# Two transformer-like layers on one core: when the third group's keys are sent, who sums two of eight output pairs, half a gram product, and eight tail tiles ahead of the experts

## What is computed

```python
xn = layernorm(x)
x  = x + causal_attention_16_heads(xn, w_qkv, w_o) + moe_top2_of_16(xn, Wg, bias, W1, W2)
xn = layernorm(x)
# second layer: no softmax; q and k are divided by their norms over all tokens
q, k, v = split(xn @ W + b)
qn, kn  = q / norm(q, over tokens), k / norm(k, over tokens)
attn    = qn * sum(kn * v, over tokens)                  # one row of 256 for all tokens
moe     = sum over the 4 best of 16 experts: weight * (silu(xn @ we1) * (xn @ we3)) @ we2
shared  = (silu(xn @ ws1) * (xn @ ws3)) @ ws2
x  = x + attn + shared / 5 + moe * 4 / 5
```

## Time and profile before

| | us |
|---|---|
| median of 3 runs | 906.23 (905.91 to 911.66) |
| the profiled execution | 906.89 |
| its span, first to last instruction | 905.2 |
| TensorE busy | 830.5 (92%) |
| VectorE busy | 645.3 (71%) |
| ScalarE busy | 468.8 (52%) |
| GpSimd busy | 437.1 (48%) |

### The profile page before, as it was taken

One profiled execution on the slowest core, in us unless ns is written; L12 is line 12 of the kernel. 1 busy time (PEld: TensorE's weight loads), 2 busy tenths in 40 slices (PEclk: granted clock), 3 DMA queues, 4 the chain that ended last, 5 costly groups with the idle time before them and its releaser, 6 DMA issues. The chain is left out here.

```text
span 905.2 us, 16683 instructions
## 1 busy us (share of the span) xinstructions
PE 830.5 (92%) x4934; PEld 449.4 (50%) x4935; DVE 645.3 (71%) x1472; ACT 468.8 (52%) x883; POOL 437.1 (48%) x720
## 2 busy tenths in 40 slices
PE   5978699999988999999999998989999989999993
PEld 3533133334533444444444432138644769888982
DVE  5587988898867888888788888437547336555648
ACT  2643154556654666666565666754313046555547
POOL 3422045603652433653435446531578848878820
PEclk9997698999998999999999999989999989999997
DMA  9654772210272121272211222325852235555566
GB/s 328 212 129 137 207 142 89 89 46 25 81 128 71 49 61 56 80 127 71 70 38 38 55 60 76 93 65 188 302 166 88 88 117 164 157 154 159 158 255 246
DMA packets 70182, 110.05 MB, mean 122 GB/s; under 512 B 16662, under 2 KB 49942, under 8 KB 69590
## 3 DMA queue, kind: packets, MB, share of 16 engines
q1 hardware_dynamic: 49430, 54.04, 22.9%
q0 software_dynamic: 16000, 45.70, 14.7%
q10 hardware_dynamic: 4672, 9.34, 3.4%
HBM read 62.53 MB, written 46.22 MB: 120 GB/s over the span
## 5 line engine op out<-in xcount | busy, mean ns | idle before, releaser
L1275 DVE TENSOR_REDUCE part_max<-ps_row 128x1 f32<-128x512 f32 (+3 forms) x560 | 353.6, 670 | 71.1 <-PE ps_row L1429 38.7
L1139 ACT ACTIVATE probs<-ps_st 128x1024 f32<-128x1024 f32 (+3 forms) x320 | 278.2, 896 | 204.6 <-PE ps_st L1408 188.2
L1333 PE MATMUL ps_o<-probs,v_all 128*17 128x512 f32 (+3 forms) x1280 | 150.4, 542 | 6.9 <-POOL probs L1009 5.6
L1429 PE MATMUL ps_row<-ks,qs 96*128 96x512 bf16 (+3 forms) x320 | 110.2, 379 | 13.7 <-DVE part_max L1275 9.3
L1429 PE MATMUL ps_row<-xt_ks,qs 96*128 96x512 bf16 (+3 forms) x320 | 104.5, 354 | 6.9 <-DVE part_max L1275 6.5
L1682 POOL DMA_INDIRECT yd<-moe_ys,moe_home x79 | 82.6, 1046 | 25.5 <-POOL moe_home L1676 13.4
L1408 PE MATMUL ps_st<-qs,ks 99*128 99x512 bf16 (+3 forms) x320 | 88.7, 360 | 2.9 <-DMA qs<-max_parts 2.7
L1408 PE MATMUL ps_st<-qs,xt_ks 99*128 99x512 bf16 (+3 forms) x320 | 85.7, 356 | 3.9 <-ACT probs L1139 2.8
L1702 PE MATMUL moe_ps_h<-moe_xs_t,moe_w_now 128*128 128x128 f32 x632 | 86.0, 280 | 1.3 <-ACT moe_xs_t L1607 0.8
L1702 PEld LDWEIGHTS moe_ps_h<-moe_xs_t,moe_w_now 128*128 128x128 f32 x632 | 78.4, 195 | 3.2 <-DVE moe_w_now L1569 2.0
L1429 PEld LDWEIGHTS ps_row<-ks,qs 96*128 96x128 bf16 x320 | 31.9, 100 | 95.6 <-DVE part_max L1275 52.8
(11 more groups left out here) (288 smaller groups left out, 1307.3 us busy)
## 6 DMA issues: line engine op xcount, KB each, us to landing
moe_xs<-xd SPq DMA_DIRECT2D x79, 129.0 KB
qk_parts<-probs SPq DMA_DIRECT2D x16, 384.0 KB, 4.2
qs<-qk_parts SPq DMA_DIRECT2D x96, 64.0 KB, 2.5
moe_xs<-xd POOLq DMA_DIRECT2D x47, 128.0 KB, 2.4
yd<-moe_ys POOLq DMA_DIRECT2D x47, 128.0 KB, 2.1
xd<-zeros POOLq DMA_DIRECT2D x2, 2048.0 KB, 15.5
moe_w<-in_w ACTq DMA_DIRECT2D x2, 2048.0 KB
w<-in_we SPq DMA_DIRECT2D x8, 512.0 KB
```

Source lines behind the costliest of these rows:

```text
L1139: act.activation(probs[:, at % NPB, :, off:CH], ps_st[at % 2][:, :, off:CH], ACT.Exp, scale=HD ** -0.5).then_inc(exp_done, 1)
L1275: dve.tensor_reduce(part_max[reduced % 2][:, h:h + k, i, j:j + 1], bank[:, 0:k * w].rearrange("p (h w) -> p h w", h=k), AX_X, ALU.max).the ...
L1333: mm = pe.matmul(ps_o[32 * q:32 * q + HD + 1, off:CH], m.v_all[:, k, g * HG + q, :], probs[:, (at + q // 2) % NPB, q % 2, off:CH], start=F ...
L1429: mm = pe.matmul(cols, qs[c][0:KROWS, h, i * P:(i + 1) * P], ks[g % 2][0:KROWS, h, j * CH:j * CH + w], start=True, stop=(j < c))
```

## The change

- SP sends the third group's keys (g = 2, buffer `ks`) right behind the unit `spread` of share 1, in place of `turn` (1, 2). Groups 1 and 3 are sent where they were.
- At the end, for the pairs 2 and 3 (`SUMMED`) ScalarE scales all four sets of blocks as before, but TensorE sums them: four products with a matrix that holds 5 on its diagonal (`five`), made by GpSimd at the start of the block, since the closing addition divides by 5. For the six other pairs ScalarE scales three sets and VectorE multiplies and adds the fourth itself (two instructions of 128 x 256). Loads and scalings go in the order of `LAST_LOADS`, additions and stores in that of `LAST_ADDS`, TensorE's work in that of `LAST_TAILS`.
- The gram product of the second half k = 1 leaves out its left 128 columns; they are the transpose of a part of the first half, which TensorE transposes and ScalarE copies after the gram. The product of the gram with the weights is done for k = 1 first, then for k = 0.
- `TAIL_FIRST` is 8: the tail of tiles 6 and 7 is computed in the second block too, in the bank `ps_o`. In the third block three pairs have a tail.

The diff, cut to its core:

```diff
@@ -882,6 +882,12 @@

+            def keys_of(g):
+                if g >= 2:
+                    sp.wait_ge(pv_done, last_pv(g - 2, C - 1))
+                load_keys(sp, m, g, slice(0, S), k_in[g % 2])
             load_first_group(sp, m, C - 1)
@@ -907,16 +913,16 @@
                     spread_divisors(sp, m, u[1])
+                    if SHARES[u[1]] == (0, 1):
+                        keys_of(2)
                 elif u[0] == "turn":
                     g, c = u[1:3]
                     if n:
                         rows_out(sp, n, c)
                     n += 1
-                    if g + 1 < NG and c == (1 if g == 0 else 2):
-                        if g >= 1:
-                            sp.wait_ge(pv_done, last_pv(g - 1, C - 1))
-                        load_keys(sp, m, g + 1, slice(0, S), k_in[(g + 1) % 2])
+                    if (g, c) in ((0, 1), (2, 2)):
+                        keys_of(g + 1)
                     if (g, c) == (1, 0):
@@ -1539,10 +1545,12 @@
         tail_done, finished = l.sem("moe1_tail_done"), l.sem("moe1_finished")
-        scaled = l.sem("moe1_scaled")
+        scaled, five_ready = l.sem("moe1_scaled"), l.sem("moe1_five_ready")
+        five = l.sb("moe1_five", [P, P])
         yg_pair = [yg8[:, 2 * n:2 * n + 2, :, :] for n in range(T // 4)] + [
             spare4[:, 2 * n:2 * n + 2, :, :] for n in range(T // 8)] + [last4[:, 2 * n:2 * n + 2, :, :] for n in range(T // 8)]
         step_sem = l.sem("moe1_dve")
+        by_act = [(n, k) for n in LAST_LOADS for k in range(top if n in SUMMED else top - 1)]
         block = ctx.enter_context(nc.Block())
@@ -1587,10 +1595,10 @@
                 sp.wait_ge(y_out[b], 16 * len(range(b, tiles, U)))
-            for n in range(T // 2):
+            for n in LAST_LOADS:
                 sp.dma_start(yg[2 * n], rows_of(2 * n)).then_inc(fetched[n], 16)
-            for n in range(T // 2):
-                sp.wait_ge(finished, n + 1)
+            for at, n in enumerate(LAST_ADDS):
+                sp.wait_ge(finished, at + 1)
                 sp.dma_start(out[0, 2 * n * P:2 * (n + 1) * P, :].rearrange("(i p) d -> p i d", p=P),
@@ -1617,11 +1625,11 @@
                 act.wait_ge(y_out[b], 16 * len(range(b, tiles, U)))
-            for n in range(T // 2):
+            for n in LAST_LOADS:
                 act.dma_start(yg[2 * n + 1], rows_of(2 * n + 1)).then_inc(fetched[n], 16)
-            for n in range(T // 2):
+            for n in LAST_LOADS:
                 act.wait_ge(fetched[n], 32)
-                for k in range(top):
+                for k in (k for pair, k in by_act if pair == n):
                     for i in (2 * n, 2 * n + 1):
@@ -1653,20 +1661,27 @@
             step = Steps(dve, step_sem)
-            for n in range(T // 2):
+            for n in LAST_ADDS:
                 both = m.x[:, 2 * n:2 * n + 2, :]
-                for k in range(top):
-                    dve.wait_ge(scaled, n * top + k + 1)
-                    step.then(dve.tensor_tensor(both, yg_pair[n][:, :, k, :], both, ALU.add))
-                if 2 * n < TAIL_FIRST:
-                    dve.sem_inc(finished, 1)
-                else:
-                    dve.wait_ge(tail_done, n + 1 - TAIL_FIRST // 2)
+                if n not in SUMMED:
+                    for k in range(top - 1):
+                        dve.wait_ge(scaled, by_act.index((n, k)) + 1)
+                        step.then(dve.tensor_tensor(both, yg_pair[n][:, :, k, :], both, ALU.add))
+                    dve.wait_ge(fetched[n], 32)
+                    for i in (2 * n, 2 * n + 1):
+                        step(dve.scalar_tensor_tensor(m.x[:, i, :], yg[i][:, top - 1, :], m.r["weight"][:, i, top - 1:top],
+                                                      m.x[:, i, :], ALU.mult, ALU.add))
+                    step.sync()
+                if n in LAST_TAILS:
+                    dve.wait_ge(tail_done, LAST_TAILS.index(n) + 1)
                     dve.scalar_tensor_tensor(both, ps_tail[n].rearrange("p (i d) -> p i d", d=D), 1.0 / (TOP1 + 1), both,
                                              ALU.mult, ALU.add).then_inc(finished, 1)
+                else:
+                    dve.sem_inc(finished, 1)

         @block.gpsimd
         def _(pool):
+            pool.tensor_scalar(five[:, :], m.ident[:, :], float(TOP1 + 1), None, ALU.mult).then_inc(five_ready, 1)
             step = Steps(pool, pool_sem)
@@ -1715,15 +1730,27 @@
             pe.wait_ge(hid_ready, tiles)
-            for n in range(TAIL_FIRST // 2, T // 2):
+            pe.wait_ge(five_ready, 1)
+            for n in LAST_TAILS:
+                bank = ps_tail[n]
                 if n == T // 2 - 2:
                     pe.wait_ge(y_copied, tiles)
                 for i in (2 * n, 2 * n + 1):
-                    mm = shared_tail(pe, m, ps_tail[n], i)
+                    if n not in SUMMED:
+                        mm = shared_tail(pe, m, bank, i)
+                        continue
+                    for k in range(top):
+                        pe.wait_ge(scaled, by_act.index((n, k)) + 1)
+                        mm = pe.matmul(bank[:, i % 2 * D:(i % 2 + 1) * D], five[:, :], yg[i][:, k, :],
+                                       start=(k == 0), stop=(k == top - 1))
                 mm.then_inc(tail_done, 1)


-TAIL_FIRST, TAIL_BEFORE = 6, 14
+TAIL_FIRST, TAIL_BEFORE = 8, 14
+SUMMED = (2, 3)
+LAST_LOADS = (0, 1, 2, 4, 5, 3, 6, 7)
+LAST_ADDS = (0, 1, 4, 2, 5, 6, 3, 7)
+LAST_TAILS = (4, 5, 6, 2, 7, 3)
 ROOT_BEFORE = 7
@@ -1756,11 +1783,11 @@
         banks_g = [l.ps(f"ps_gram{b}", [P, CH]) for b in range(KH)]
-        ps_g = [b[:, 0:DP] for b in banks_g]
+        ps_g = [b[:, k * P:DP] for k, b in enumerate(banks_g)]
         bank_l = l.ps("ps_l2", [P, CH])
         ps_ab = [l.ps(f"ps_ab{b}", [P, CH]) for b in range(2)]
         ps_o = l.ps("ps_o2", [P, 2, D])
-        ps_tail = [banks_g[1], banks_g[0], bank_l]
+        ps_tail = [banks_g[1][:, :], banks_g[0][:, :], bank_l[:, :], ps_o[:, :, :].rearrange("p i d -> p (i d)")]
         ps_gw, ps_sums, ps_ones = banks_g, bank_l, banks_g[0]
@@ -1881,7 +1908,9 @@
             for k in range(KH):
-                act.copy(gram[:, k, :], ps_g[k]).then_inc(gram_copied, 1)
+                act.copy(gram[:, k, k * P:DP], ps_g[k]).then_inc(gram_copied, 1)
+            act.wait_ge(gram_done, 2)
+            act.copy(gram[:, 1, 0:P], banks_g[0][:, 0:P]).then_inc(xt_ready, 1)
             act.wait_ge(logit_ready, 1)
@@ -1999,8 +2028,8 @@
                 dve.wait_ge(b_in, 16)
-                for k in range(KH):
-                    dve.wait_ge(gw_done, k + 1)
+                for k in (1, 0):
+                    dve.wait_ge(gw_done, KH - k)
                     step(dve.tensor_tensor(prod[:, k, 0:2 * D], ps_gw[k][:, :], w[:, k, 0:2 * D], ALU.mult))
@@ -2080,7 +2109,7 @@
                 pair = m.x[:, 2 * b:2 * b + 2, :]
-                step(dve.scalar_tensor_tensor(pair, bank[:, :].rearrange("p (i d) -> p i d", d=D), 1.0 / (TOP1 + 1), pair,
+                step(dve.scalar_tensor_tensor(pair, bank.rearrange("p (i d) -> p i d", d=D), 1.0 / (TOP1 + 1), pair,
                                               ALU.mult, ALU.add))
@@ -2115,7 +2144,7 @@
                     for k in range(KH):
-                        mm = pe.matmul(ps_g[k], xn[:, i, k * P:(k + 1) * P], xn[:, i, 0:DP],
+                        mm = pe.matmul(ps_g[k], xn[:, i, k * P:(k + 1) * P], xn[:, i, k * P:DP],
                                        start=(i == 0), stop=(i == T - 1))
@@ -2186,7 +2215,10 @@
             pe.wait_ge(gram_copied, KH)
-            for k in range(KH):
+            pe.transpose(banks_g[0][:, 0:P], gram[:, 0, P:2 * P], m.ident[:, :]).then_inc(gram_done, 1)
+            for k in (1, 0):
+                if k == 0:
+                    pe.wait_ge(xt_ready, T + 1)
                 for j in range(KH):
                     mm = pe.matmul(ps_gw[k][:, :], gram[:, j, k * P:(k + 1) * P], w[:, j, 0:2 * D],
                                    start=(j == 0), stop=(j == KH - 1))

```

## The result

The changed kernel is slower by 0.6%: over 15 runs of each, interleaved on one chip, the ratio of its time to that of the kernel before is 1.0059, 95% interval 1.0035 to 1.0084 (medians 915.62 and 907.40 us; executions in a disturbed state of the chip are in the medians and left out of the ratio). That is +3.2 to +7.6 us; forecast were +7.9, with "within 1%" as the likeliest class and 909.0 to 918.5 us as the range. On 906.23 us the ratio gives 911.6 us: class and range hold, and the point lies 2.5 us too high. The profiled execution after took 910.74 us, span 909.0, against 906.89 and 905.2.

The account below looks back on a forecast made before the run. TensorE was taken to bound attention, and the chain load, scale, add, store the end. Keys +9.9, boundary +0.4 and end -2.4 made +7.9 on 906.2: 914.1 us, range 909.0 to 918.5 us.

Parts of the forecast that it names:

- Part 1, the keys: Attention: later third-group keys remove TensorE's 6.0 us stop but add one of 15.9 us, net +9.9 us (+1.3 to +11.3).
- The rival of the fast keys: Attention: with TensorE stopped, keys land 5.7 us after first issue, new stop 7.3 us, total 905.5 us; chance 0.09.
- the 5.6 us: Attention: time for the six key loads by the skill's rule, 2.0 us plus bytes at 436 GB/s, making the edit nearly free.
- The old stop: Attention, kernel before: TensorE stands 6.00 us until 274.19 because the first divisors' gather queues behind six key loads; expected to go.
- the slow stretches behind the two stops cancel: Attention: TensorE's half-clock time after the new stop taken as long as after the old, worth 2.6 us, so no net term.
- Part 2, the half gram: Second block: shorter gram passes save 3.5 us of TensorE, of which -2.1 us net is kept (0 to -3.3).
- Part 3, the tail tiles: End of second block: two more tiles add 5.2 us of TensorE, using up VectorE's cover before SP's last load; +0.4 us (0 to +2.8).
- the cover of 2.6 us is used up, +0.4 us: Second block's end: VectorE's last product moves from 727.98 to 731.1 against SP's last load at 730.61, costing +0.4 us.
- Part 4, the end: Last stretch: less scaling and adding, ScalarE fed by the loads, VectorE ends at 900.1 instead of 902.59; -2.4 us.
- The rival of full length: Keys take their 15.7 us (+11.3), boundary +1.5, end gives 2.0: +10.8, total 917.0 us; chance 0.17.
- that of no gain at the end: Last stretch: pairs 2 and 3 wait on ScalarE and TensorE, VectorE idles what it saves; total 916.5 us; chance 0.10.
- that of no stop: Attention: SP reaches the spread earlier, so the new TensorE stop does not happen; total 895.6 us; chance 0.04.

Follow-up runs that it names:

- the first three groups: Three of four follow-up sets of kernels, each measured together with the kernel before, which took 907 to 918 us in the first and 896 to 897 in the others.
- the pair of the third group: The kernel before and the changed kernel, both measured again together: ratios 0.9997 and 1.0078, medians 896.72 and 904.95 us.
- the first group: Changed kernel with third group's keys at the old place, 0.999; kernel before with the keys' edit alone, 1.002; changed kernel with keys behind the first gather, 0.989.
- the second and third group: Sets with kernel before plus idle products (0.9993), eight tail tiles (1.0018) or half gram (0.9985), changed kernel unsummed (1.0110); then both kernels, each also with keys behind first gather (0.9858, 0.9866).
- the run without sums: Changed kernel with no pair summed by TensorE, pairs in the order 0 to 7: ratio to the kernel before 1.0110 [1.0085, 1.0135].
- The second measurement: The changed kernel unaltered, measured again against the kernel before: ratio 1.0078 [1.0052, 1.0104], median 904.95 us.

## Why the prediction was right, and where it was not

**Part 1, the keys: right.** The two terms are 16.11 and 6.00 us; I had 15.9 and 6.0. The landing took 14.4 us, and I had 14.3. That it came so close is partly luck: the two instances gave 15.7 and 15.5 us, and the 1.3 us that I took off for the experts' traffic came from no row. That these loads fill the DMA engines by themselves is shown by the rows with all compute engines stopped. The rival of the fast keys falls, and with it the 5.6 us. The Trainium skill (DMA: Bandwidth & Descriptors, Anatomy of one DMA) states the rule behind those 5.6 us for one DMA of GpSimd's path; these are six on SP's queue, and their 14.4 us don't agree with it. Three more profiles with this edit, one of each of the first three groups, have stops of 15.66, 16.30 and 17.01 us. The old stop is less steady, 4.45 to 7.36 us over the six profiles that have it. That the slow stretches behind the two stops cancel holds nearly: the clock came back 5.2 us after the restart before and 4.3 after, worth 0.5 us, and in the other profiles 3.3 to 3.9 us after the old stop and 3.6 to 6.2 after the new one.

Attention as a whole became only 8.4 us longer, though SP's marks were late by 9.8 until 576 us: some 1.4 us came back in the last 30 us of the stage. In the pair of the third group attention is 10.0 longer, in that of the first 6.0. The difference lies in slow stretches behind 500 us. Their length times what PEclk lacks to 1.00 is an estimate of their cost: 3.4 us before and 1.7 after, 3.4 and none in the first group, 3.4 and 3.4 in the third. Without them attention is longer by 10.1, 9.4 and 10.0 us, and my +9.9 is what the keys cost. Why a profile has one, two or no such stretches stays open.

**Part 2, the half gram: right.** -2.3 us at the gram's end, before the transpose, as worked out. At the boundary it is worth 2.2 us: with eight tail tiles VectorE ends 128.1 us into the block with it and 130.3 without. By itself it moves the kernel by less than the measurement tells (0.9985 [0.9964, 1.0006]), since GpSimd's scatters and SP's loads ended the block before.

**Part 3, the tail tiles: right in size, by a different last engine.** From the start of the block VectorE ends at 128.1 us instead of 125.2: +2.9, of the +3.1 that -2.1 + 5.2 make. SP's last load ends at 125.5 instead of 127.8, since the 64 scatters took 63.8 us instead of 65.8. I had them as long as before, and VectorE's end within 0.5 us of SP's; they are 2.6 us apart. Whether the change has a part in this is open: of the profiles read here, six of the seven with the half gram have 63.6 to 64.0 us of scatters and one has 66.7; five of the six without have 65.6 to 66.5 and one has 63.8. The boundary moved by +0.2 against +0.4, since before SP set it and now VectorE does. Had SP ended as early before, the two tiles would have cost over 2 us.

**The experts: the term that was missing.** I had costed nothing behind the boundary, and a gap of over 1 us there, which I had named as a sign of being wrong, is in the trace: 1.35 us. But filling the 4.10 us at the barrier has a second effect: TensorE's clock. It was at 1.2 GHz for the experts' first products before and at 2.4 GHz after, and the experts are 2.8 us shorter. The profiles of the second and third group show 1.1 to 2.2 us for it, between profiles of one group at 1.00 and at 0.66 to 0.79; the rest of the 2.8 stays open, and since the stage took 130 to 143 us over the groups, this is the weakest of the accounts. This step, "the cover of 2.6 us is used up, +0.4 us", counted the cover only as room, and not as idle time that costs clock behind it. It is the largest part of the distance between +7.9 and the +3.8 of the profiles.

**Part 4, the end: right in size, in part by another wait.** -2.1 against -2.4. The sums are in time and VectorE ends, as written. But I had ScalarE fed by the loads up to the last pair, and it waits for them only ahead of the first three. The end of the run without sums is 2.1 us longer, so the gain hangs on them.

**The whole.** The second measurement, 1.0078, is +7.0 us, that of the first +5.3; both intervals overlap. The rival of full length (+10.8) and that of no gain at the end fall by the landing of 14.4 us and by the end that is 2.1 us shorter, that of no stop by the 16.11 us.

What the prediction did not ask is whether the old stop needed a late place to go away. The gather was late because six slow loads stood ahead of it in the queue, so it was enough to let it pass, with 39 us left until the keys are read. The change moved them behind five more steps of the divisors' chain (return 0 to spread 1), 41 us further.

## What to carry to other kernels

- When a small transfer on which a chain hangs waits behind a large one in the same queue, swap the two first. Moving the large one further costs up to its whole length once its reader comes before its landing; here the swap alone was worth 1.3%, and the change with the longer move, its other gains included, cost 0.6 to 0.8%.
- Take a load's length from an instance of the same shape in the trace, here 14 to 16 us for six times 256 KB, and check its slack: landing against the first read.
- Idle time ahead of a stretch that TensorE bounds can be paid twice, once as the wait and once as slow products behind it, so count both when work is moved into such a gap. Here the second part was 1.1 to 2.2 us between profiles, too little for a ratio to show.

## What the runs showed of the hardware that was not expected

- Six loads of 256 KB, each to 16 partitions, keep the 16 DMA engines full (share 1.03 to 1.05) at 129 to 133 GB/s with all compute engines idle. They take 14.4 us so, and 15.2 us with TensorE at work. Why they are that slow wasn't tried.
- A small gather (128 x 32 float32) lands 13.8 us after its issue behind these loads, and 2.0 us after it just ahead of them in the queue.
- Behind an idle time of 1.35 us at the barrier TensorE's clock stayed at 2.4 GHz in two profiles and was down to a mean of 0.79 over the next 8 us in three; behind 1.68 us it stayed in one. Behind 3.99 to 5.05 us it was down to 0.66 to 0.79 in all six.
- The same 64 scatters of GpSimd took 63.6 to 66.7 us in all, from one profile to another, and the experts' stage 130 to 143 us.
